# Another order of a mixer step: projection before ranks, a copy and the exponentials earlier, x1 before the positions

## The reference

```
h = layernorm(x) * (1 + ca) + sa
x = x + ga * mixer(h)          # a state space mixer (Mamba 2 kind)
h = layernorm(x) * (1 + cb) + sb
x = x + gb * experts(h)        # 64 experts, 8 picked for each token, and a shared one
```

## Time and profile before

| what | value |
|---|---|
| median of 3 executions | 6409.54 us (6404.81 to 6410.18) |
| the profiled execution | 6412.97 us, its span 6411.1 us |
| mixer stage | about 200 to 3200 us of the span |
| mean granted clock of PE over the span | 0.951 of 2.4 GHz |

### The profile page before, as it was taken

How to read it: one execution, slowest core, us unless ns; L and a number is a source line. 1 busy time by engine, 2 the same in 40 slices (tenths; PEclk the granted TensorE clock), 3 DMA queues, 4 the chain that set the end, 5 groups by cost and what they waited for, 6 DMA issues and landing times. The chain is left out here.

```text
span 6411.1 us, 109995 instructions
## 1 busy us (share of the span) xinstructions
PE 5781.9 (90%) x28797; PEld 4345.1 (68%) x28798; DVE 3957.1 (62%) x10033; ACT 2733.7 (43%) x5780; POOL 3763.9 (59%) x2980
## 2 busy tenths in 40 slices
PE   2888888888888888888859999999999999999899
PEld 0556555565565565565548888888788888888787
DVE  1888888888888888888834444444344444444355
ACT  1555555555555555555513333333333333333322
POOL 0466666666666666666645555555555555555477
PEclk8899999999999999999979999999999999999999
DMA  9243343333343333333348887887877777887687
GB/s 351 107 124 119 106 131 120 111 130 107 117 136 105 119 125 105 122 122 105 129 123 194 196 217 173 213 196 175 228 155 176 186 164 179 211 214 196 106 269 256
DMA packets 338146, 1028.39 MB, mean 160 GB/s; under 512 B 55060, under 2 KB 59412, under 8 KB 337124
## 3 DMA queue, kind: packets, MB, share of 16 engines
q1 hardware_dynamic: 175512, 669.44, 30.3%
q0 software_dynamic: 145568, 321.56, 25.7%
q10 hardware_dynamic: 16816, 34.37, 1.4%
HBM read 580.45 MB, written 444.74 MB: 160 GB/s over the span
## 5 line engine op out<-in xcount | busy, mean ns | idle before, releaser
L1324 POOL DMA_INDIRECT acc_dram<-y_e,ids x576 | 907.9, 1576 | 1115.6 <-ACT y_e L1397 680.3
L1205 PE MATMUL bank<-w_hi,x_hi 128*128 (+1 forms) x2560 | 1058.0, 413 | 0.0
L1205 PE MATMUL bank<-w_hi,x_lo 128*128 (+1 forms) x2560 | 1002.3, 392 | 0.0
L1205 PE MATMUL bank<-w_lo,x_hi 128*128 (+1 forms) x2560 | 1001.5, 391 | 0.0
L938 DVE SCALAR_TENSOR_TENSOR acc<-raw,conv_w,acc 128x128 f32<-128x128 f32 x1920 | 820.3, 498 | 7.3 <-ACT acc L665 7.3
L602 POOL DMA_INDIRECT list_dram<-tok_id,pos x512 | 633.3, 1237 | 155.9 <-issue 154.6
L1415 DVE TENSOR_TENSOR h_lo<-bank,h_hi 128x256 fp32r<-128x256 f32 x576 | 243.5, 423 | 753.5 <-ACT h_hi L1386 746.8
L1397 ACT ACTIVATE y_e<-bank,xg_e 128x512 f32<-128x512 f32 x576 | 396.4, 688 | 693.4 <-PE bank L1205 649.1
L1316 POOL DMA_INDIRECT xg_e<-h_dram,ids x576 | 572.0, 993 | 195.0 <-issue 174.1
L1391 ACT ACTIVATE th_f<-bank 128x256 f32<-128x256 f32 x576 | 221.3, 384 | 1017.6 <-PE bank L1205 964.1
L770 PE MATMUL bank<-xn_t,w_in 128*128 128x128 f32 x5120 | 590.5, 277 | 66.4 <-ACT xn_t L644 66.4
(11 more groups left out here) (248 smaller groups left out, 10997.2 us busy)
## 6 DMA issues: line engine op xcount, KB each, us to landing
hi_dram<-w_hi_m SPq DMA_DIRECT2D x130, 768.0 KB, 7.4
lo_dram<-w_raw SPq DMA_DIRECT2D x130, 768.0 KB, 8.8
w_hi<-hi_dram SPq DMA_DIRECT2D x130, 768.0 KB
w_lo<-lo_dram SPq DMA_DIRECT2D x130, 768.0 KB
w_raw<-in_w_experts_dram SPq DMA_DIRECT2D x128, 768.0 KB
acc_dram<-zeros ACTq DMA_DIRECT2D x2, 16640.0 KB, 102.5
acc_c<-acc_dram SPq DMA_DIRECT2D x128, 256.0 KB, 3.5
h_dram<-h SPq DMA_DIRECT2D x64, 288.0 KB
```

The costliest lines, as they stand in the source:

```text
L1205: last = nc.tensor.matmul(acc, a, b, start=(i == 0), stop=(i == len(terms) - 1))
L1324: pool.indirect_dma_start(acc_dram[r % NACC], bass.IndirectOffsetOnAxis(ap=ids[:, r:r + 1], axis=0), y[:, r % YSLOTS, :], None, compute_op ...
```

## The change

On PE, the output projection (L842) moves ahead of the two rank matmuls. On ACT, the copy `y_t` moves from the end of the step to in front of the square of y, and the two exponentials move in front of hn2. On DVE, the block of the positions moves from in front of the second `split_lo` and x1 to behind x1 and its statistics, the end of the step.

```diff
 ACT
+                    if c is not None:
+                        for j in range(2):
+                            act.wait_ge(S["rows_ps"], 2 * c + j + 1)
+                            nc.scalar.activation(lm[:, j * DI:(j + 1) * DI], (bank[3] if j == 0 else bank[1])[:], ACT.Exp).then_inc(S["l_exp"], 1)
                     if t is not None:
                         act.wait_ge(S["ln2_stat"], t + 1)
                         at_least(act, S["h2_done"], t)
                         nc.scalar.activation(hn2[:], x1[:, 1 - p, :], ACT.Identity, bias=nm2[:], scale=rs2[:]).then_inc(S["hn2_done"], 1)
-                    if c is not None:
-                        for j in range(2):
-                            act.wait_ge(S["rows_ps"], 2 * c + j + 1)
-                            nc.scalar.activation(lm[:, j * DI:(j + 1) * DI], (bank[3] if j == 0 else bank[1])[:], ACT.Exp).then_inc(S["l_exp"], 1)
...
                     if c is not None:
+                        act.wait_ge(S["yT_ps"], c + 1)
+                        at_least(act, S["out_ps"], c)
+                        nc.scalar.copy(y_t[:].rearrange("p k t -> p (k t)"), bank[2][:]).then_inc(S["yT_sb"], 1)
+                    if c is not None:
                         act.wait_ge(S["y_done"], c + 1)
                         at_least(act, S["r2_done"], c)
                         nc.scalar.activation(junk[:], y[:], ACT.Square, accum_out=ssq2[:]).then_inc(S["ssq2_done"], 1)
...
-                    if c is not None:
-                        act.wait_ge(S["yT_ps"], c + 1)
-                        at_least(act, S["out_ps"], c)
-                        nc.scalar.copy(y_t[:].rearrange("p k t -> p (k t)"), bank[2][:]).then_inc(S["yT_sb"], 1)
 PE
+                    if c is not None:
+                        pe.wait_ge(S["yT_sb"], c + 1)
+                        pe.wait_ge(S["yoff_sb"], c + 1)
+                        for i in range(KI):
+                            last = nc.tensor.matmul(half(7), y_t[:, i, :], w_out[:, i, :], start=(i == 0), stop=(i == KI - 1))
+                        last.then_inc(S["out_ps"], 1)
                     if t is not None:
                         pe.wait_ge(S["picked_done"], t + 1)
                         if c is not None:
                             pe.wait_ge(S["yadd_done"], c + 1)
                         nc.tensor.matmul(half(2)[:, 0:EXPERTS], tri_bf[:], picked[:], start=True, stop=True)
                         nc.tensor.matmul(half(2)[:, EXPERTS:2 * EXPERTS], ones_bf[:], picked[:], start=True, stop=True).then_inc(S["rank_ps"], 1)
-                    if c is not None:
-                        pe.wait_ge(S["yT_sb"], c + 1)
-                        pe.wait_ge(S["yoff_sb"], c + 1)
-                        for i in range(KI):
-                            last = nc.tensor.matmul(half(7), y_t[:, i, :], w_out[:, i, :], start=(i == 0), stop=(i == KI - 1))
-                        last.then_inc(S["out_ps"], 1)
 DVE
-                    if t is not None:
-                        dve.wait_ge(S["rank_ps"], t + 1)
...
-                        tt(nbase[:], nbase[:], half(2)[:, EXPERTS:2 * EXPERTS], ALU.subtract).then_inc(S["rank_done"], 1)
...
-                        ts(pos[:, 1 - p, :], kmax[:], -1.0, float(KEY), ALU.mult, ALU.add).then_inc(S["pos_done"], 1)
                     if ws is not None:
                         split_lo(dve, ws, 1)
                     if c is not None:
                         dve.wait_ge(S["out_ps"], c + 1)
...
                         ts(ve2[:], mv2[:, 1:2], LN_EPS, None, ALU.add).then_inc(S["ln2_var"], 1)
+                    if t is not None:
+                        dve.wait_ge(S["rank_ps"], t + 1)
...
+                        tt(nbase[:], nbase[:], half(2)[:, EXPERTS:2 * EXPERTS], ALU.subtract).then_inc(S["rank_done"], 1)
...
+                        ts(pos[:, 1 - p, :], kmax[:], -1.0, float(KEY), ALU.mult, ALU.add).then_inc(S["pos_done"], 1)
```

More of the change, by code:

```diff
@@ L1044, in step @@
                                 in1=half(j), op0=ALU.add, op1=ALU.mult).then_inc(S["gz_done"], 1)
-                    if t is not None:
-                        dve.wait_ge(S["rank_ps"], t + 1)
-                        place.mark(stt(out=key[:], in0=half(2)[:, 0:EXPERTS], scalar=-1.0, in1=nbase[:], op0=ALU.mult, op1=ALU.add))
-                        tt(nbase[:], nbase[:], half(2)[:, EXPERTS:2 * EXPERTS], ALU.subtract).then_inc(S["rank_done"], 1)
[L1049 to L1056, removed]
-                        ts(pos[:, 1 - p, :], kmax[:], -1.0, float(KEY), ALU.mult, ALU.add).then_inc(S["pos_done"], 1)
                     if ws is not None:
@@ L1076, in step @@
                         ts(ve2[:], mv2[:, 1:2], LN_EPS, None, ALU.add).then_inc(S["ln2_var"], 1)
+                    if t is not None:
+                        dve.wait_ge(S["rank_ps"], t + 1)
+                        place.mark(stt(out=key[:], in0=half(2)[:, 0:EXPERTS], scalar=-1.0, in1=nbase[:], op0=ALU.mult, op1=ALU.add))
+                        tt(nbase[:], nbase[:], half(2)[:, EXPERTS:2 * EXPERTS], ALU.subtract).then_inc(S["rank_done"], 1)
+                        at_least(dve, list_st[1 - p], 16 * TOPK * (t // 2))
+                        ts(tok_id[:, 1 - p:2 - p], tok_id[:, 1 - p:2 - p], 2.0 * P, None, ALU.add)
+                        place.wait()
+                        place.mark(tt(key[:], key[:], picked[:], ALU.mult))
+                        place.wait_apart(passed)
+                        place.mark(nc.vector.max(out=kmax[:], in_=key[:]))
+                        place.wait()
+                        place.end()
+                        ts(pos[:, 1 - p, :], kmax[:], -1.0, float(KEY), ALU.mult, ALU.add).then_inc(S["pos_done"], 1)
                 steps(dve, step)
```

## The result

The changed kernel takes 6445.37 us (median of 5 executions, 6443.16 to 6448.27); the kernel before took 6409.37 us beside it on the same chip. The ratio is 1.0057, 95% interval 1.0046 to 1.0069: slower by 36 us. The forecast was 6484 us, +74. Direction and place came as forecast, and the mechanism in the main, at a little under half the size. The profiled execution took 6448.27 us, its span 6446.5.

What follows compares the result with a forecast made beforehand. The mixer was taken as bound by a loop of waits through several engines. 62 full steps at +1.2 us gave 74 us; 6409.5 + 74 = 6484 us, own range 6440 to 6550, 8 in 10 for 6405 to 6575.

Steps and rivals of the forecast that it cites:

- Steps 1 to 3: PE and DVE: projection 1.97 us earlier; x1 2.7 to 3.6 earlier; L736 waits for ranks, 0.4 us gain left at best.
- case B: Clock falls before the projection and again behind the ranks' wait; L770 at 22.2, +1.5 to +2.3 us a step.
- Step 4: PE behind the ranks' wait: clock falls, costing 2.0 or 1.7 us (0 to 2.40); L770 at 21.6 or 22.2.
- case A: Clock falls behind the ranks' wait instead of before the projection; L770 at 21.6, +0.9 to +1.6 us a step.
- +1.2 us, the middle of A: Later of the paths through PE and POOL to the convolution's second half: +1.2 us on each of 62 steps, 74 us.
- Step 5: ACT: exponentials 21.5 to 23.4, L913 from 22.5 but not passed on; hn2 at 23.4, POOL's `nm` ends 30.7 to 31.9.
- Step 6: ACT and POOL: square 2.1 us later, statistics 1.3 later, hn2 possible from 22.7, covered since hn2 isn't reached before 23.4.
- The delays of the list: POOL's list transfers beside both L481s on DVE: a second delay for sure, 1.55 us, left out of the sum.
- third rival: POOL becomes the bound through its late list, or the clock falls twice: +2.3 to +3.5 us a step, 6552 to 6627; chance 0.17.
- first rival: Clock stays up from L736 to L770: at best -1.1 us a step, 6341 to 6397 us; chance 0.09.
- one for one swap: Clock costs about 1 us behind the wait, POOL is quicker: -0.3 to +0.4 us a step, 6391 to 6434; chance 0.12.

Runs made afterwards that it cites:

- list first: POOL's eight list transfers moved in front of its wait for the square; 6417.35 us on the changed kernel, 6407.1 us on the kernel before.
- e13: Changed kernel plus useless matmuls in PE's waits: one before y's transposes, one behind them, four behind the ranks; 6382.33 us.
- e4: Changed kernel with the exponentials behind hn2 on ACT again; 6455.56 us.
- e9: Changed kernel with POOL's eight list transfers in front of its wait for the square, the ranks' wait kept; 6417.35 us.
- e1: Changed kernel with the positions in front of x1 again on DVE, behind the low half of the weights; 6413.86 us.
- e2: Changed kernel with the ranks written into the second half of bank 2, so x's transposes don't wait for them; 6457.23 us.
- e3: Changed kernel plus four useless matmuls behind the ranks, to keep the clock up through the ranks' wait; 6420.4 us.
- e11: Kernel before plus four useless matmuls a step in PE's waits, one ahead of y's transposes and three behind; 6335.49 us.
- e10: e7 plus four useless matmuls a step inside PE's waits, in all three places where the clock fell; 6234.51 us.
- e7: Changed kernel with the ranks in bank 2's second half and POOL's list transfers in front of its wait for the square; 6387.03 us.
- e8: Kernel before with only POOL's eight list transfers moved in front of its wait for the square; 6407.1 us.

## Why the prediction was right in kind and half in size

*Steps 1 to 3 held.* Projection at 2.19 (forecast 2.18), x1 at 10.03 (10.1), L736 at 13.09 (13.1), in case B 14.14 (14.0). That this wait is a loss by itself is shown by the right-hand column: with POOL out of the way by list first, the changed order takes 6319 and the old one 6258, and the new order without the wait 6235. So the wait costs 85 us there, and the rest of the new order is worth 23 (the filler of the three stands in other places, so both are rough).

*Step 4 was right in kind, too large in case A.* In 39 of 60 steps the clock fell where it was forecast, at a price of 1.66 us where I took 2.0: from L736 to L770 went 8.05 us, 6.39 of them without the fall (e13; forecast 6.5). L770 came at 21.14, not 21.6. Case B came as written, L770 at 22.23 (22.2) and L938's second half at 34.3 (34.2), but in 7 steps only. In 9 the clock stayed up behind the wait, and in 5 the fall cost 3.3 us (9.70 less 6.39), above the 2.40 that step 4 had as its most.

*The step that failed is the sum's "+1.2 us, the middle of A".* The mean step became longer by 0.67 us. The middle was made of a path through PE at +0.9 and a path through POOL that reached to +1.6, for all steps alike. POOL's path was not the later one in case A: `nm` ended at 30.00, not at 30.7 to 31.9, since h2 (L554) started at 23.71, not 24.3, and from there to the end of `nm` POOL took 6.29 us, not 6.4 to 7.58; hn started 0.77 behind it, after ACT's own taps. PE's path brought L938's second half to 33.19, not 33.6, which is +0.48 in place of +0.9, and from L938 to y it took 14.96, 0.12 less than before, where I had "unchanged". What is left is +0.36, the 48.15 of most steps. Kinds 3 and 4, +1.33 and +2.10 in 12 steps of 60, bring the mean to +0.67. I had A and B as alternatives for the whole kernel; they alternate within it, with two kinds that the forecast did not have. What decides the kind of a step was not followed up.

*Step 5 held in its times.* L913 starts at 22.05 (22.5 forecast), hn2 1.45 later than before. That the earlier L913 "isn't passed on" was not quite so: by e4 the exponentials' place is worth some 10 us.

*Step 6 ("that covers it") held in case A and failed in kind 2.* In the step shown the statistics come at 22.10, before hn2's turn. In kind 2 they come at 23.85, not the 22.7 of step 6, and hn2 waits for them; list first takes 0.7 us off such a step and 28 us off the kernel. So POOL's price, left out of the sum, is not zero.

*The delays of the list.* By the Trainium skill, "SBUF — State Buffer", under the diagram of the ports, the prediction had the lock of the port pair delay a second transfer for sure. Both L481s did meet the list, but not at 1.55 us each: beside the second a transfer took 2.38, beside the first one took 0.96 (it began 0.06 ahead of L481) and the next 1.37. The other long ones are the 2.29 beside the product at L1016 and the 1.88. The list took longer, 15.0 from r2's start to its end where it was 13.2. But L612 and L547 behind it took 1.27 and 0.57 where they had taken 2.67 and 1.64, beside a DVE that was waiting (the 4.15 us in front of L913), as the third rival's counter-argument had it. POOL paid the list's delay and got most of it back: the statistics were there 0.8 later than before (22.10 against 21.33), where step 6 had 1.3 and the third rival 2.8 to 4.4; in kind 2 it is 2.5.

*The rivals.* The clock stayed up behind the wait in 9 steps of 60, and in them POOL kept the step at 48.2 (47.53 without it, e9). (With hn2 at 22.7 the first rival's way through POOL gives 33.6 by the terms of step 5, not 33.2; nothing rests on it.) The one for one swap was missed by 11 us. POOL as the bound is not what set most steps of the changed kernel, but it is why undoing the ranks' wait gives nothing beyond par (e1), and it holds e13 and, in front of ACT's copies, e2. Two chains of nearly one length stood beside each other, and taking away one gave 25 to 32 us (e1, e3, e9), whichever it was.

*The clock.* It costs 73 us in the kernel before (e11) and 63 in the changed one (e13); the change moved it and saved little. These prices are rough, since the filler takes PE's time itself and shifts the instructions behind it.

## What to carry to other kernels

Before moving a producer back in an in-order queue, look up who next needs its buffer: the ranks' bank was free almost five us early, and after the move over three us late. Where the granted clock is under 1.00 in every step, price a rearrangement with the clock kept up too (filler in the waits is a quick test); otherwise what the order gives, the clock takes back at another place. And when undoing a loss gives only the loss, look for the chain right behind it: here only both together, and the filler, gave 2.7 to 3.3%.

## What the runs showed that I had not expected

**Matmuls that nobody reads made every kernel faster**: by 73 us in the kernel before (e11), 63 in the changed (e13), 153 in e10 against e7, with 4 to 6 of them in each step's waits.

**Steps settle at the same length in different kernels.** The kernel before, e1, e2, e3, e7 and e8 have long stretches of steps of 47.8 us, though their waits differ, and only with the clock at 1.00 do they part (46.57 to 44.35). e2 has stretches at another such length; of one step of 51.23, from 2481.85, PE's order in time:

```profile
2518.35 6.93 PE L813 MATMUL bank<-x1s,lm 128*128 128x64 f32 x32
2525.07 8.17 PE L822 MATMUL bank<-w_in,xn_t 128*128 128x512 f32 x16
```

L813 takes 6.93 where the changed kernel needs 3.68, and L822 8.17 for 7.08: in that stretch the fall comes at a third place (granted clock 0.50 from 2518 to 2525). Why steps settle at these lengths stays open: no run here separates a cause from chance.
